# An image-and-graph kernel whose squares are taken from the rectified tile, with its engine work laid out by thirds of steps and its row gathers split anew

## The chip, the cores and the metric

The kernel runs on one core of a Trainium2 chip. The metric is the device time of one execution in microseconds (us), the median of several runs. The engines of the core work side by side and meet through semaphores: TensorE (PE in the rows, PEld for its weight loads) multiplies matrices into PSUM, VectorE (DVE) and ScalarE (ACT) do elementwise work, GpSimd (POOL) issues the row gathers through its own DMA queue, and SyncE (SP) issues the plain transfers.

## What is computed

The input is 32 images of 64 channels and 48 x 48 pixels. First comes a "convolution" by similarity, per image, then a mixture of experts whose gates come from a graph attention over all pixels. Cut to what matters:

```
xf = ln_c(x)                                            # per pixel over the 64 channels
xn = xf / |xf|
s  = relu(einsum('bcp,bcq->bpq', xn, xn)) ** 2          # 2304 x 2304 per image
g  = Wc xf + bc
x  = x + einsum('bpq,bcq->bcp', s, g)
t  = tokens of x;  n = ln_t(t)
h  = n @ W_gat                                          # 16 values per token, 4 heads
e  = leaky_relu(a_src[src] + a_dst[dst])                # 262144 edges and one loop per token
alpha = softmax of e over the edges of each dst;  agg = segment_sum(h[src] * alpha)
gates = softmax of the top 2 of 4 experts by layernorm(agg)
x  = t + sum_e gates_e * (gelu(n W1_e + b1_e) W2_e + b2_e)
```

## The kernel before

**Stages.** From 0 to about 1409 us the edges are sorted by destination (VectorE, with TensorE and ScalarE turning and copying), woven with the first 8 images. From 1409 to 3647 us run the other 24 images. Then comes the scan over the sorted edges in 32 chunks of 82 x 128 rows (to about 4255 us), a short repair of the seams, and from about 4310 us the experts, image by image.

**The image loop.** `walk` runs one `body` per image on every engine. An image has `STEPS` = 45 steps: 5 column blocks (four of 512 pixels, one of 256) times 9 pairs of row blocks. In step t TensorE writes the gram product of a pair (L1876: 8 matmuls of 64 columns, f16 high and low words) into one of two PSUM banks, ScalarE copies it rectified into SBUF as `rel` (L2066), and a third of the steps (t % 3 = 0) are squared on ScalarE (L2070), the others on VectorE (L2406: the PSUM bank times `rel`). Three steps later (`LAG`) TensorE multiplies the squares with the value rows (`values`, L1830). The bank of step t is used again in step t + 2, and TensorE waits there for whoever read it last: ScalarE's `a_rel` where ScalarE squares, VectorE's `v_s2` elsewhere. `rel` has 3 buffers, the squares have 5.

Between the steps, tied to numbers of t by small tables, stands the work of the neighbouring images: `post` and `tokens` for the image before (products for the graph features, normalisation by `spread2`, `deviation2`, `norm2`, transposes, copies), `pre`, `spread`, `deviation`, `scales`, `norm`, `units`, `high`, `low`, `turn` and `value_rows` for the image behind, `sums` for each finished column block, and in the first 16 bodies after the first the scan's move masks, `level` (L2350 to L2353, byte tiles).

**GpSimd's queue.** Independent of the images GpSimd issues 2048 gathers (L980, `gather_rows`), each 128 rows of 24 floats by a list of indices in SBUF, at most four in flight; after every 64 the rows of a chunk are stored (`store_rows`, L959). The edges only name tokens of the first 8 images, so that the gathers may run while the other 24 are computed. 48 gathers are issued before this stage (`OPENING`), the rest of `AHEAD * 64` in one go; then the queue waits for the end of the images (`img_done`). In the scan, for each chunk k, `segment_rows` fetches two large tiles (`got` L1716, `nb` L1718) and `PIECE` more gathers follow. Ahead of every fourth chunk the queue first makes sure that enough gathers are issued: `full * 64 + 10`, with `full` = 6, 11, 16, 21, 26, 31 and 32 for k = 0, 4, 8, 12, 16, 20 and 24 on, and that the stores of `full` chunks have landed. ScalarE lays `nb` and `got` out (`AE`, `GT`), VectorE runs its chain of copies and scans over them.

Of the kernel before, what the change touches and what calls it, by code (L numbers as in the profile page):

```python
# [26 lines left out]
FIRST = 8  # L27
# [1210 lines left out]
def flow(nc, n, Wc, bc, Wg, att_s, att_d, b_gat, gamma, beta, W1, b1, W2, b2):  # L1238
# [42 lines left out]
    AHEAD = 29  # L1281
    PIECE = 8
# [10 lines left out]
    with ExitStack() as ctx, ExitStack() as early, ExitStack() as late:  # L1293
# [200 lines left out]
        POST_PE = {5 + 2 * i: i for i in range(NB)}  # L1494
        POST_ACT = {6 + 2 * i: i for i in range(NB)}
        PRE_PE = {19 + 2 * i: i for i in range(NB)}
        PRE_ACT = {20 + 2 * i: i for i in range(NB)}
# [267 lines left out]
        def _(pe):  # L1765
            n.merge_tensor(pe)
            def pre(b, par, i):

                if i == 0:
                    at_least(pe, n.a_tn, NB * (b - 1))  # L1770
                else:
                    pe.wait_ge(n.a_cv, NB * b + i)
# [8 lines left out]
            def turn(b, i):  # L1781

                q0, k = TBATCH[i]
                if i == 0:
                    pe.wait_ge(n.v_lo, b + 1)
                if i >= 2:
                    pe.wait_ge(n.a_hl, NTB * b + i - 1)
# [74 lines left out]
            def body(b, own, par, nth, before, more, moved=None):  # L1862
                pe.wait_ge(n.l_in[par], 32 * (nth + 1))
                for t in range(STEPS):
                    c, k = divmod(t, PAIRS)
                    o, w = CH[c]
                    if t % 3 == 2:
                        pe.wait_ge(a_rel, STEPS * own + (t - 1))
                    else:
                        at_least(pe, v_s2, by_dve(STEPS) * own + by_dve(t - 1))  # L1870
# [12 lines left out]
                    if before and t in POST_PE:  # L1883
                        post(b - 1, 1 - par, POST_PE[t])
                    if before and t == 15:
                        tokens(b - 1, 0)
                        tokens(b - 1, 1)
                    if before and t == 17:
                        tokens(b - 1, 2)
                    if more and t in PRE_PE:  # L1890
                        if t == 19:
                            pe.wait_ge(n.x_in[1 - par], 64 * (nth + 1 + par))
                        pre(b + 1, 1 - par, PRE_PE[t])
                    if more and t == 33:
                        turn(b + 1, 0)
                        turn(b + 1, 1)
                    if more and t == 35:
# [55 lines left out]
        def _(act):  # L1953
            n.merge_scalar(act)

            def pre(b, i):
# [34 lines left out]
            def post(b, i):  # L1991
# [6 lines left out]
                for h in range(2):  # L1998
                    act.activation(c2[:, s0:s0 + k, h, :], src[:, h], ACT.Copy)
                for h in range(2):  # L2000
# [682 lines left out]
```

## Time and profile before

| | |
|---|---|
| median of 3 runs | 5282.03 us (5274.48 to 5291.11) |
| profiled execution | 5291.28 us, its span 5289.5 us |
| gathers begin | 1126.4 us |
| the 24 images, first to last gram product | 1408.8 to 3629.1 us |
| last token store of the images | 3647.2 us |
| GpSimd's first `got` of the scan | 3658.6 us |
| last of the 2048 gathers | 4102.0 us |
| `got` of chunk k = 24 | 4111.1 us |
| end of the span | 5289.5 us |

Busy shares of the span: PE 67%, VectorE 75%, ScalarE 64%, GpSimd 56%. They are averages over stages with different limits. In such a profile the question is at each meeting point who came last; an engine that is busy all the time in one stage may still have room against another queue that runs beside it through several stages.

### The profile page before, as it was taken

What the parts mean: (1) busy time and instruction counts of PE and PEld (TensorE: products, weight loads), DVE (VectorE), ACT (ScalarE), POOL (GpSimd) and SP (SyncE); (2) the same over time, 40 slices, a digit from 0 to 9 for tenths busy, and PEclk for the clock granted to TensorE, in tenths of its full rate; (3) what the DMA queues carried; (4) which work ended last, traced back from release to release, by engine and by line L of the source; (5) the groups of instructions that cost most, each with busy time, mean ns of one, the idle gap of its engine ahead of it and who ended that gap; (6) DMA issues with size and microseconds to landing.
All of it is one profiled execution on the core that took longest, in us unless ns stands there. A gap on an engine that the chain in (4) does not pass through costs nothing. (4 is left out here: it accounts for less than half of the span.)

```text
span 5289.5 us, 70597 instructions
## 1 busy us (share of the span) xinstructions
PE 3533.1 (67%) x22687; PEld 1450.6 (27%) x22687; DVE 3964.2 (75%) x5512; ACT 3392.4 (64%) x4285; POOL 2941.6 (56%) x2937
## 2 busy tenths in 40 slices
PE   4888988500488888888898988884000017788778
PEld 1223333200243344343443444342000002222222
DVE  8998988997666666766666655555999848787877
ACT  4777988401676767776676776775566526566665
POOL 6000000048777777777777777777656147666661
PEclk9999999755699999999999999997555558888889
DMA  6100100002122222222222212224555527999997
GB/s 258 36 20 20 33 21 16 17 14 82 22 47 57 42 62 48 47 52 52 56 48 46 64 40 53 48 50 105 176 190 187 190 71 147 151 161 159 155 157 141
DMA packets 332482, 441.96 MB, mean 84 GB/s; under 512 B 183193, under 2 KB 261916, under 8 KB 331500
## 3 DMA queue, kind: packets, MB, share of 16 engines
q1 hardware_dynamic: 209744, 288.12, 19.8%
q0 software_dynamic: 105536, 148.61, 16.6%
q8 instruction: 187, 3.06, 0.2%
q10 hardware_dynamic: 16896, 1.18, 0.2%
q14 instruction: 119, 0.97, 0.1%
HBM read 252.35 MB, written 166.47 MB: 79 GB/s over the span
## 5 line engine op out<-in xcount | busy, mean ns | idle before, releaser
L980 POOL DMA_INDIRECT rows<-htab_d,idx x2048 | 2134.3, 1042 | 761.3 <-issue 603.9
L2406 DVE SCALAR_TENSOR_TENSOR s<-gram,rel 128x1024 f32<-128x1024 f32 (+1 forms) x720 | 798.1, 1116 | 800.1 <-ACT rel L2066 797.3
L2066 ACT ACTIVATE rel<-gram 128x1024 f32<-128x1024 f32 (+1 forms) x1080 | 1005.4, 940 | 540.5 <-PE gram L1876 533.1
L1830 PE MATMUL acc<-s,gT 128*64 128x512 f32 (+1 forms) x4320 | 1020.2, 552 | 0.0
L1876 PE MATMUL gram<-hl 128*64 128x512 f16 (+1 forms) x4320 | 787.9, 367 | 217.5 <-DVE s L2406 182.3
L1876 PE MATMUL gram<-hl,lh 128*64 128x512 f16 (+1 forms) x4320 | 775.5, 361 | 13.5 <-issue 13.5
L1761 POOL DMA_INDIRECT R<-seg_d,nidx x576 | 587.7, 1020 | 191.3 <-issue 165.9
L1930 PE MATMUL ye<-hid,w 128*64 128x384 f32 x1536 | 376.2, 570 | 260.5 <-DVE ms L2625 195.8
L1080 POOL IOTA slots<- 64x2048 int32 x1 | 1.8, 1833 | 975.5 <-POOLq L192 975.5
L2158 ACT ACTIVATE hid<-up,b1t 128x768 f32<-128x768 f32 x384 | 333.8, 900 | 261.4 <-PE up L1942 260.1
L1876 PEld LDWEIGHTS gram<-hl 128*64 128x64 f16 x4320 | 244.5, 110 | 708.2 <-DVE s L2406 467.3
L1913 PE MATMUL tailsT<-ident,tails 128*20 128x128 f32 x24 | 5.2, 412 | 610.6 <-DVE tails L2513 610.6
L906 ACT ACTIVATE w_s2r<-w_gram 128x1024 f32<-128x1024 f32 (+1 forms) x360 | 349.4, 971 | 94.0 <-PE w_gram L775 93.5
L316 DVE TENSOR_TENSOR edges<-edges 128x2048 f32<-128x2048 f32 (+1 forms) x186 | 370.8, 1994 | 47.7 <-ACT edges L935 42.1
L1942 PE MATMUL up<-tne,w 64*128 64x384 f32 x1536 | 397.7, 599 | 3.1 <-DMA x2e<-x_d 2.5
L317 DVE TENSOR_TENSOR edges<-edges 128x2048 f32<-128x2048 f32 (+1 forms) x186 | 369.7, 1987 | 0.0
L888 ACT ACTIVATE w_s2r<-w_s2r 128x1024 f32<-128x1024 f32 (+1 forms) x360 | 362.1, 1006 | 0.0
L749 PE MATMUL w_acc<-w_s2r,w_gT 128*64 128x512 f32 (+1 forms) x1440 | 361.2, 581 | 1.1 <-ACT w_s2r L888 1.1
L2070 ACT ACTIVATE s<-rel 128x1024 f32<-128x1024 f32 (+1 forms) x360 | 349.8, 972 | 11.5
L2625 DVE SCALAR_TENSOR_TENSOR ms<-ye,b2c,gs 128x384 f32<-128x384 f32 x384 | 232.0, 616 | 152.2 <-PE up L1942 92.3
L1830 PEld LDWEIGHTS acc<-s,gT 128*64 128x64 f32 x4320 | 298.8, 138 | 155.8 <-issue 3.3
L1876 PEld LDWEIGHTS gram<-hl,lh 128*64 128x64 f16 x4320 | 246.3, 111 | 236.9 <-issue 134.5
(372 smaller groups left out, 5401.4 us busy)
## 6 DMA issues: line engine op xcount, KB each, us to landing
gs<-gates_d SPq DMA_DIRECT2D x64, 1024.0 KB
rows<-htab_d,idx POOLq DMA_INDIRECT x2048
seg_d<-state SPq DMA_DIRECT2D x32, 996.0 KB, 8.9
raw_d<-w_zeros POOLq DMA_DIRECT2D x48, 512.0 KB, 23.2
raw_d<-rows POOLq DMA_DIRECT2D x32, 768.0 KB
tne<-tn_d SPq DMA_DIRECT2D x32, 576.0 KB
x2e<-x_d SPq DMA_DIRECT2D x32, 576.0 KB
out<-res SPq DMA_DIRECT2D x64, 256.0 KB
```

Of the source, the lines that this page charges most:

```text
L316: dve.tensor_tensor(lo, a, b, ALU.min)
L317: step(dve.tensor_tensor(hi, a, b, ALU.max))
L749: last = pe.matmul(acc[(b + c) % 2][j * C:(j + 1) * C, 0:w], gT[:, b % 2, 2 * k + j, :], s2(s)[:, j * w:(j + 1) * w], start=k == 0, stop=k ...
L888: act.activation(s2(s)[:, 0:2 * w], rel(s)[:, 0:2 * w], ACT.Square).then_inc(a_s2, 1)
L980: pool.indirect_dma_start(out=n.rows[:, k % 2, j, :], out_offset=None, in_=n.htabx, in_offset=bass.IndirectOffsetOnAxis(ap=n.idx[:, g % 2, ...
L1761: pool.indirect_dma_start(out=R[:, par, j, :], out_offset=None, in_=n.seg, in_offset=bass.IndirectOffsetOnAxis(ap=nidx[:, par, j:j + 1], a ...
L1830: last = pe.matmul(acc[(par + c) % 2][j * C:(j + 1) * C, 0:w], gT[:, par, 2 * k + j, :], s2[:, u % SLOTS, j * w:(j + 1) * w], start=k == 0 ...
L1876: last = pe.matmul(bank[h * C:(h + 1) * C, j, 0:w], word[:, par, first_pixel:first_pixel + C], hl[:, par, o:o + w], start=own_words, stop= ...
L1930: last = pe.matmul(y[i % 2][h * C:(h + 1) * C, 0:EW], w2[:, k, :], hid[:, i % GROUP, h, :], start=True, stop=True)
L1942: last = pe.matmul(up[i % GROUP][:, h, 0:EW], w1[rows_, k, :], tne[rows_, par, cp * EW:(cp + 1) * EW], start=True, stop=True)
L2066: act.activation(rel[:, t % RELS, 0:2 * w].rearrange("p (j x) -> p j x", j=2), gram[(par + t) % 2][:, :, 0:w], ACT.Relu, scale=1.0 / SPLIT ...
L2406: dve.scalar_tensor_tensor(halves(s2[:, t % SLOTS, 0:2 * w]), gram[(par + t) % 2][:, :, 0:w], 1.0 / SPLIT ** 2, halves(rel[:, t % RELS, 0: ...
```

## The change

Squares: VectorE squares `rel` by itself (both inputs the same SBUF tile) in place of multiplying the PSUM bank with `rel`. With that the bank is free after ScalarE's copy, and TensorE waits for `a_rel` in every step. Order: the work beside the steps gets new places, on VectorE almost all of it at t % 3 = 0, where VectorE has no square; `sums`, `level`, `post`, `pre`, `tokens` and the rest move; `value_rows` is cut in two (`value_scaled` at t = 36, `value_rows` at t = 0 of the next body). ScalarE's `pre` and `post` copy both halves in one instruction in place of two. Gathers: `AHEAD` goes from 29 to 26 and `PIECE` from 8 to 13.

```diff
-    AHEAD = 29
-    PIECE = 8
+    AHEAD = 26
+    PIECE = 13
...
-        POST_PE = {5 + 2 * i: i for i in range(NB)}
-        POST_ACT = {6 + 2 * i: i for i in range(NB)}
-        PRE_PE = {19 + 2 * i: i for i in range(NB)}
-        PRE_ACT = {20 + 2 * i: i for i in range(NB)}
+        POST_AT = {5 + 3 * i: i for i in range(NB)}
+        PRE_AT = {14 + 3 * i: i for i in range(NB)}
...
-                    if t % 3 == 2:
-                        pe.wait_ge(a_rel, STEPS * own + (t - 1))
-                    else:
-                        at_least(pe, v_s2, by_dve(STEPS) * own + by_dve(t - 1))
+                    at_least(pe, a_rel, STEPS * own + (t - 1))
...
+                    if before and t == 23:
+                        if more:
+                            pe.wait_ge(n.a_cv, NB * (b + 2))
                         tokens(b - 1, 0)
...
                 if i == 0:
                     at_least(act, n.v_t, b)
+                    at_least(act, n.v_g, b)
...
-                for h in range(2):
-                    act.activation(dst(cv)[:, h], src[:, h], ACT.Copy)
-                for h in range(2):
-                    last = act.activation(dst(sq)[:, h], src[:, h, :, 0:C], ACT.Square)
-                last.then_inc(n.a_cv, 1)
+                act.activation(dst(cv), src, ACT.Copy)
+                act.activation(dst(sq), src[:, :, :, 0:C], ACT.Square).then_inc(n.a_cv, 1)
...
-            LEVEL_AT = {9: 0, 15: 1, 18: 2, 24: 3, 33: 4, 36: 5, 42: 6}
+            LEVEL_AT = {6: 0, 9: 1, 12: 2, 15: 3, 21: 4, 27: 5, 42: 6}
+            SUMS_AT = {12: 0, 21: 1, 33: 2, 39: 3}
...
+            def value_scaled(b):
+                dve.tensor_tensor(vr[:, :, :], cv[:, :, C:2 * C], wide(rstd[:, :]), ALU.mult).then_inc(n.pc, 1)
+
             def value_rows(b, par):
-
-                dve.tensor_tensor(vr[:, :, :], cv[:, :, C:2 * C], wide(rstd[:, :]), ALU.mult).then_inc(n.pc, 1)
                 dve.wait_ge(n.pc, b + 2)
...
                         dve.wait_ge(a_rel, STEPS * own + t + 1)
-                        halves = lambda ap: ap.rearrange("p (j x) -> p j x", j=2)
-                        dve.scalar_tensor_tensor(halves(s2[:, t % SLOTS, 0:2 * w]), gram[(par + t) % 2][:, :, 0:w], 1.0 / SPLIT ** 2,
-                                                 halves(rel[:, t % RELS, 0:2 * w]), ALU.mult, ALU.mult).then_inc(v_s2, 1)
+                        dve.tensor_tensor(s2[:, t % SLOTS, 0:2 * w], rel[:, t % RELS, 0:2 * w], rel[:, t % RELS, 0:2 * w], ALU.mult).then_inc(v_s2, 1)
...
+                    if before and t == 0:
+                        value_rows(b, par)
...
+                    if more and t == 36:
+                        value_scaled(b + 1)
```

On TensorE, in an image's body, two steps stand in a row like this before (`misc` is the bank of `pre`; the names behind "waits" are semaphores):

```order
L1876 MATMUL gram<-hl 64x512 [waits v_s2]
L1876 MATMUL gram<-hl 64x512
L1876 MATMUL gram<-hl,lh 64x512 x2
L1876 MATMUL gram<-hl 64x512 x2
L1876 MATMUL gram<-hl,lh 64x512 x2
L1824 REGISTER_ALU [waits v_s2]
L1830 MATMUL acc<-s,gT 64x512 [waits a_s2]
L1830 MATMUL acc<-s,gT 64x512
```

and now:

```order
L1872 MATMUL gram<-hl 64x512 [waits a_rel]
L1872 MATMUL gram<-hl 64x512
L1872 MATMUL gram<-hl,lh 64x512 x2
L1872 MATMUL gram<-hl 64x512 x2
L1872 MATMUL gram<-hl,lh 64x512 x2
L1822 REGISTER_ALU
L1829 MATMUL acc<-s,gT 64x512 [waits a_s2,v_s2]
L1829 MATMUL acc<-s,gT 64x512
```

The products and their number stay; the first gram product waits for ScalarE's copy, and VectorE's square is waited for only by the value products three steps later.

On VectorE, where an image's statistics are made (`ssq` is `spread`, `rstd` to `n` is `scales`, `vr` and `gT` are the value rows), before:

```order
L2406 SCALAR_TENSOR_TENSOR s<-gram,rel 128x1024 [waits a_rel]
L2267 RECIPROCAL rstd<-sd 128x18 [waits a_sd]
...
L2270 TENSOR_SCALAR n<-n 128x18 [waits v_chain]
...
L2406 SCALAR_TENSOR_TENSOR s<-gram,rel 128x1024 [waits a_rel]
L2362 TENSOR_TENSOR vr<-cv,rstd 128x1152
...
L2364 TENSOR_TENSOR gT<-vr,bcb 128x1152 [waits pc]
```

and now:

```order
L2402 TENSOR_TENSOR s<-rel 128x1024 [waits a_rel]
...
L2402 TENSOR_TENSOR s<-rel 128x1024 [waits a_rel]
L2261 RECIPROCAL rstd<-sd 128x18 [waits a_sd]
...
L2264 TENSOR_SCALAR n<-n 128x18 [waits v_chain]
L2345 TENSOR_SCALAR step_m<-step_d 128x328
...
L2402 TENSOR_TENSOR s<-rel 128x1024 [waits a_rel]
...
L2402 TENSOR_TENSOR s<-rel 128x1024 [waits a_rel]
```

The squares come in pairs and read SBUF alone; the other work stands behind each pair, and the value rows have left this place.

On GpSimd, at the end of the gathers (the row of 54 lies ahead of k = 20), before, from k = 21 on:

```order
L1716 DMA got<-raw_d,edge 128x1968
L1718 DMA nb<-htab_d,node 128x1992
L980 DMA rows<-htab_d,idx 128x24 x8
...
L980 DMA rows<-htab_d,idx 128x24 x8
L959 DMA raw_d<-rows 128x1536
L1716 DMA got<-raw_d,edge 128x1968
```

and now, from the end of k = 19 to k = 20:

```order
L980 DMA rows<-htab_d,idx 128x24 x10
L959 DMA raw_d<-rows 128x1536
L980 DMA rows<-htab_d,idx 128x24 x54
L968 TENSOR_LOAD need
L968 ISA x2
L980 DMA rows<-htab_d,idx 128x24 x10
L959 DMA raw_d<-rows 128x1536
L1714 DMA got<-raw_d,edge 128x1968
L1716 DMA nb<-htab_d,node 128x1992
L980 DMA rows<-htab_d,idx 128x24 x13
```

192 gathers have moved from ahead of the first `got` to between the chunks, 5 more to each and 70 in a row ahead of the `got` of k = 20, with the store of the 31st chunk directly ahead of it.

## Rows read from the trace of the kernel before

**Rows 1.** Head of the page.

```profile
span 5289.5 us, 70597 instructions
```

**Rows 2.** Waits of POOL: engine, line <- releaser: us in total, times, longest us.

```profile
POOL rows L980 <- issue: 603.9, 1930, 6.1
...
POOL rows L980 <- DMA rows<-htab_d,idx: 157.5, 118, 5.1
...
POOL got L1716 <- ACT GT L2111: 83.1, 6, 16.5
```

**Rows 3.** Gathers until 3411 and until 3658: count, ns min/median/max, first and last start.

```profile
L980 POOL DMA_INDIRECT rows<-htab_d,idx x1665: 942/947/7027, 1126.4 to 3411.0; - x185
...
L980 POOL DMA_INDIRECT rows<-htab_d,idx x1856: 942/947/7027, 1126.4 to 3657.4; - x186
```

**Rows 4.** Timeline at the images' end: start us, us, engine, line, operation.

```profile
3647.16 0.33 SPq L1588 DMA_DIRECT2D tn_d<-tf  x1
...
3658.60 0.95 POOL L1716 DMA_INDIRECT got<-raw_d,edge  x1 [0.30 <-issue]
```

**Rows 5.** Start of the chain that ended last: start us, us, what.

```profile
4105.51 5.55 issue
...
4111.06 0.96 POOL got L1716
...
4112.33 7.57 DMA nb<-htab_d,node
...
4119.92 1.04 ACT AE L2110
```

**Rows 6.** Gram matmuls (L1876): count, ns min/median/max, first and last start.

```profile
L1876 PE MATMUL gram<-hl x4320: 272/379/636, 1408.8 to 3629.1; 128*64 128x512 f16 x157, 128*64 128x256 f16 x40
```

**Rows 7.** Timeline, two steps of an image, TensorE.

```profile
2303.85 0.11 PEld L1876 LDWEIGHTS gram<-hl 128*64 128x64 f16 x2 [0.72 <-DVE s L2406]
...
2305.60 0.38 PE L1876 MATMUL gram<-hl 128*64 128x512 f16 x2
```

**Rows 8.** Waits, 1450 to 3600 us.

```profile
PEld gram L1876 <- DVE s L2406: 451.2, 441, 2.8
```

**Rows 9.** Groups by form, 1409 to 3632 us: count | busy us, mean ns | idle before.

```profile
L980 POOL DMA_INDIRECT rows<-htab_d,idx x1670 | 1659.1, 993 | 544.6 <-issue 484.8 <-DMA rows<-htab_d,idx 59.8
...
L2406 DVE SCALAR_TENSOR_TENSOR s<-gram,rel 128x1024 f32<-128x1024 f32 x576 | 703.1, 1223 | 749.2 <-ACT rel L2066 748.7 <-issue 0.2
```

**Rows 10.** The same, 3042 to 3632 us.

```profile
L980 POOL DMA_INDIRECT rows<-htab_d,idx x456 | 445.1, 976 | 140.1 <-issue 134.5 <-DMA rows<-htab_d,idx 5.6
```

**Rows 11.** Timeline, gathers beside VectorE's merge (L1152 to L1154 without pause).

```profile
1131.88 1.96 POOL L980 DMA_INDIRECT rows<-htab_d,idx  x1 [0.30 <-issue]
...
1131.80 1.21 DVE L1154 TENSOR_TENSOR edges<-edges 128x1024 f32<-128x1024 f32 x1
...
1135.40 1.96 POOL L980 DMA_INDIRECT rows<-htab_d,idx  x1 [0.30 <-issue]
```

**Rows 12.** Timeline, gathers beside two VectorE operations of an image.

```profile
2314.47 1.64 POOL L980 DMA_INDIRECT rows<-htab_d,idx  x1 [0.30 <-issue]
...
2313.94 1.35 DVE L2362 TENSOR_TENSOR vr<-cv,rstd 128x1152 f32<-128x1152 f32 x1
...
2303.21 0.95 POOL L980 DMA_INDIRECT rows<-htab_d,idx  x1 [0.30 <-issue]
...
2302.57 1.22 DVE L2406 SCALAR_TENSOR_TENSOR s<-gram,rel 128x1024 f32<-128x1024 f32 x1 [1.22 <-ACT rel L2066]
```

**Rows 13.** Timeline, one chunk of the scan.

```profile
3788.42 0.95 POOL L1716 DMA_INDIRECT got<-raw_d,edge  x1 [0.30 <-issue]
...
3799.88 2.79 POOL L980 DMA_INDIRECT rows<-htab_d,idx  x1 [3.94 <-DMA rows<-htab_d,idx]
...
3798.30 3.62 DVE L2505 TENSOR_TENSOR_SCAN S<-G 128x1660 f32<-128x1660 f32 x1
...
3806.89 0.96 POOL L1716 DMA_INDIRECT got<-raw_d,edge  x1 [0.30 <-issue]
```

More of the change, by code:

```diff
@@ L1769, in pre @@
                 if i == 0:
-                    at_least(pe, n.a_tn, NB * (b - 1))
+                    at_least(pe, n.a_c2, NB * (b - 1))
                 else:
@@ L1785, in turn @@
                     pe.wait_ge(n.v_lo, b + 1)
+                    at_least(pe, n.a_tn, NB * (b - 1))
                 if i >= 2:
@@ L1997, in post @@
                 src = misc[:, :, 0:k * PW].rearrange("p h (s c) -> p h s c", c=PW)
-                for h in range(2):
-                    act.activation(c2[:, s0:s0 + k, h, :], src[:, h], ACT.Copy)
-                for h in range(2):
-                    last = act.activation(sq2[:, s0:s0 + k, h, :], src[:, h, :, 0:C], ACT.Square)
-                last.then_inc(n.a_c2, 1)
+                by_half = lambda t: t[:, s0:s0 + k, :, :].rearrange("p s h c -> p h s c")
+                act.activation(by_half(c2), src, ACT.Copy)
+                act.activation(by_half(sq2), src[:, :, :, 0:C], ACT.Square).then_inc(n.a_c2, 1)
             def deviation2(b):
@@ L2070, in body @@
                         act.activation(s2[:, t % SLOTS, 0:2 * w], rel[:, t % RELS, 0:2 * w], ACT.Square).then_inc(a_s2, 1)
-                    if before and t in POST_ACT:
-                        post(b - 1, POST_ACT[t])
-                    if before and t == 12:
+                    if before and t in POST_AT:
+                        post(b - 1, POST_AT[t])
+                    if more and t in PRE_AT:
+                        pre(b + 1, PRE_AT[t])
+                    if before and t == 17:
                         deviation2(b - 1)
-                    if before and t == 16:
+                    if before and t == 23:
                         tokens(b - 1, 0)
                         tokens(b - 1, 1)
-                    if before and t == 18:
+                    if before and t == 26:
                         tokens(b - 1, 2)
-                    if more and t in PRE_ACT:
-                        pre(b + 1, PRE_ACT[t])
-                    if more and t == 26:
+                    if more and t == 25:
                         deviation(b + 1)
@@ L2085, in body @@
                         norm(b + 1)
-                    if more and t == 30:
+                    if more and t == 32:
                         high(b + 1)
-                    if more and t == 34:
+                    if more and t == 35:
                         turned(b + 1, 1 - par, 0)
                         turned(b + 1, 1 - par, 1)
-                    if more and t == 36:
+                    if more and t == 37:
                         turned(b + 1, 1 - par, 2)
@@ L2397, in norm2 @@
                 dve.tensor_tensor(hx[:, 16:18, :], c2[:, 8, :, C:PW], r[:, 8, :].unsqueeze(2).to_broadcast([P, 2, RW]), ALU.mult).then_inc(n.v_t2, 1)
+            value_scaled(FIRST)
             value_rows(FIRST, 0)
@@ L2419, in body @@
                         scales(b + 1)
-                    if more and t == 28:
-                        value_rows(b + 1, 1 - par)
-                    if more and t == 29:
+                    if more and t == 30:
                         units(b + 1)
-                    if more and t == 31:
-                        low(b + 1)
+                    if more and t == 36:
+                        value_scaled(b + 1)
                     if moved and t in LEVEL_AT:
```

30 lines of the change are left out of this document (15 added, 15 removed).

## The prediction

> **What bounds the kernel now.** (GpSimd is POOL in the rows.) I read the page first for the busy shares, then the chain that ended last, the waits of GpSimd, and the timeline at the places they name. TensorE, VectorE and ScalarE are busy nine tenths or less of the image phase and wait for each other there: TensorE lost 451 us before its gram products because VectorE still read the bank [rows 8]. It looks like the bound. The chain says otherwise. It starts at 4105.5 us in GpSimd's queue: the 25th chunk's fetch (`got`, k = 24) starts at 4111.1, its neighbour rows land 7.6 us later, ScalarE lays them out, and from there VectorE's scan chain runs to the end [rows 5]. So ask what GpSimd did until then. It issued 2048 gathers, and its idle time before them is 0.3 us of issue (603.9 us in 1930 times) and waits for landed rows (157.5 us); it waited for a consumer six times only, after the last gather [rows 2]. It never waited for an image. The images are over at 3647.2, and GpSimd takes its first `got` at 3658.6, when its 29 x 64 = 1856 gathers are issued [rows 3, 4]. **GpSimd's queue sets the time from 1126 to 4111 us; the images have 11 us to spare beside it.** A gather that nothing disturbs takes 0.95 us and 0.30 of issue: 1.25 us.
>
> **The image loop.** The change frees a gram bank after ScalarE's rectified copy instead of after VectorE's product. TensorE's own step is 1.75 us (2303.85 to 2305.60, the second start kept by no engine) [rows 7]; 36 wide steps of 1.75 and 9 half-width ones of about 0.9 make 71 us, some 7 us of other products and transposes 78. An image takes (3629.1 - 1408.8) / 24 = 92.5 us now [rows 6]. With small stalls left I estimate 82, so the images end near 1409 + 24 x 82 + 18 = 3395 (18 being 3647.2 - 3629.1, the last image's end work). That is 250 us off TensorE and nothing off the path, since GpSimd needs until 3411 for the 26 x 64 = 1664 gathers at its old pace [rows 3]. The work laid out by thirds is the same work on VectorE and TensorE, and ScalarE's merged copies move the same elements; at most a few us per image come off ScalarE. The added waits are met long before: ScalarE's first copy of an image (t = 14) waits for the value rows that VectorE now finishes at t = 0, with 14 steps between; TensorE's first token transpose (t = 23) waits for ScalarE's copy of t = 20, with the gram products of step 24 queued behind it and three steps, over 5 us, of room. SyncE's stores of an image follow five to eight steps later in unchanged order, and nothing but the last image's end work waits for them. All this I cost at nothing on the path. Its cover is the gather queue: without that, the images would bring the 250 us.
>
> **The squares.** 30 of 45 steps per image are squared on VectorE. Before, this read PSUM and one SBUF tile, 1.22 us each, 576 wide ones [rows 9]. Now it reads the SBUF tile twice. A product of two SBUF tiles of 128x1024 takes 1.21 us [rows 11], so VectorE pays nothing. GpSimd does. A gather that starts 0.64 us into the old form (2303.21 against 2302.57) still takes 0.95 us; one that starts 0.53 us into a product of two SBUF tiles (2314.47 against 2313.94) takes 1.64 and ends 0.82 us after that product [rows 12]. Beside the merge, one that starts 0.08 us in takes 1.96 and ends 0.83 us after the product [rows 11]. So a gather held inside such an operation goes on when it ends.
>
> The Trainium skill says the same on the page "SBUF — State Buffer" (Who interferes with whom): a VectorE instruction with two SBUF inputs contends with a GpSimd instruction that reads SBUF, and the loser waits in full. By that rule the squares hold gathers. The same section infers that descriptor generation needs the write side and so is not stalled by a two-tensor product; by that the squares would cost nothing (the first rival). The rows above decide between the two, and against the second.
>
> Price of one wide square to the gather queue. From below: two squares of a third sit 1.3 us apart, a held gather restarts in step, and each costs 0.03 to 0.05. From above: at steps of 1.75 a held gather restarts 2.34 us after the square's start (1.22 + 0.82 + 0.30), inside the second square, and again 1.75 later, and then 1.25 later it falls into the next third; three gathers per 5.25 us, 1.5 us lost to two squares, 0.75 each. Between: beside the merge two gathers take 3.52 us (1131.88 to 1135.40) where 2.50 would do, 1.02 lost to three operations, 0.34 each [rows 11]. And from 3042 to 3632, where no level work runs, gathers average 976 ns against 947 undisturbed [rows 3, 10]: 456 x 0.029 = 13 us for 6.4 images with five two-tile operations of 1.35 us each, 0.41 per operation. Both are near each other and of the same kind, so I take **0.35 us**. For 576 wide squares (24 images of 24) that is 202 us, for 144 half-width ones at an estimated 0.06 another 9: **+211 us** on the gather queue. Bounds: 17 to 29 us (0.03 to 0.05 x 576), and 432.
>
> So the scan may start at 3411 + 211 = **3622** instead of 3658.6, long after the images' 3395.
>
> **The scan with 13 gathers per chunk.** From `got` to `got` it takes 3806.89 - 3788.42 = 18.47 us now: ten issues of 1.25, a wait of 3.9 for rows that land behind the two large fetches, 1.9 held by the long scan, the rest small [rows 13]. Five more gathers add 6.25: 24.7 us. From below 15 x 1.25 + 3.9 = 22.7, if the hold falls within the landing wait; from above 26.5, if the long scan (3.62 us) holds a second issue. I take 24.7. VectorE's chain of 18.4 us then waits for each chunk. The counts: k = 0 to 19 take 260 gathers, to 1924; at k = 20 the code wants 31 x 64 + 10 = 1994 first, so 70 gathers stand ahead of that `got` (88 us), and the store of the 31st chunk behind them is waited for (6 us, as from 4105.5 to 4111.1 now [rows 5]); k = 20 to 23 take 52; the last two and the last store about 10. Sum: 24 x 24.7 + 88 + 6 + 4 = **691 us**, the 4 being what this last end takes beyond the one that is in today's count. Before: 4111.1 - 3658.6 = 452.5. The rest from k = 24 on is the same work in the same order.
>
> `got` of k = 24 then starts at 3622 + 691 = 4313 against 4111.1: **+202 us**. The gathers moved out of the image phase take back what the earlier start gives: 192 of them, 248 us earlier, 239 us more later. Against the profiled execution's span of 5289.5 us [rows 1] (its time is 5291.3) this gives 5491; the median of the runs shown, 5282.0, lies 9 us lower: 5282 + 202 = 5484 us.
>
> **Rivals.**
> (A) A square of one tile with itself does not hold the gathers, as a second read of the same address might not. No row shows this form with a gather inside, against it stands that every form with two SBUF inputs in the rows holds. Then the scan starts at 3411 and `got` 24 at 4102: -9 us, 5273, no measurable difference.
> (B) Faster. As A, and the hold by the long scan also falls within the landing wait, so that a chunk takes 22.7 us: 24 x 2.0 = 48 us less, 5225. It decides from a chunk period under about 24.4 us with squares that hold nothing. For it: in the landing wait GpSimd has 3.9 us per chunk to hide in. Against it: the rows of the squares' kind.
> (C) The squares hold gathers but fall in step with them at 0.05 each: 29 us instead of 211, 5302. For it: three gathers to a pair of squares can settle; against it the two groups of rows that measured 0.34 and 0.41.
> (D) The images do not shorten, because ScalarE or the new third-steps take the place of the wait. Then they end at 3647, GpSimd's 3622 is no longer last, and the scan starts at about 3650: +230 us, 5512.
>
> **How the numbers follow.** Forecast 0.74; A 0.10, B 0.05, C 0.05, D 0.06. Within the forecast the price per square is open from about 0.15 (-115 us) to 0.55 (+115), the chunk period by -48 and +43. D is inside. A range from 5340 to 5620 holds forecast and D up to a tail of 0.04 at each side of what I believe and leaves out A, B and C. Differences under 0.3% (16 us) can't be told by a measurement of this kernel. Faster by more: B, with a sliver of A, 0.06. Within: most of A and a little of C, 0.11. Slower by more: the forecast, D and most of C, 0.83.
>
> **What the changed profile would show.** Images: last gram matmul near 3380, TensorE hardly waiting for VectorE. Squares: mean gather above 1.2 us in the image phase (993 ns now), gathers that start inside a square ending 0.82 us after it. GpSimd's first `got` near 3620, more than 150 us after the last token store. Scan: `got` to `got` near 24.7 us, a gap of some 115 us before k = 20, `got` 24 near 4313, and the same 1178 us from there to the end. Wrong would be: gathers of 0.95 us inside squares (A), a first `got` right behind the images (D), or a chain that no longer passes through `got` 24.

## The result and the profile after

The changed kernel takes **5382.7 us** (median; 5372.2 to 5386.9) against 5282.9 us of the kernel before in the same session: a ratio of **1.0186**, interval 1.0163 to 1.0209. That is +100 us, in the forecast's direction and inside its range (5340 to 5620), but just under half of the +202 us forecast. The profiled spans differ by 5385.1 - 5289.5 = 95.6 us; the sums below are made against that.

Below, the head of the profile's page of after (the changed kernel), and the group of its gathers (line, engine, operation, count | busy us, mean ns | idle before):

```profile
span 5385.1 us, 70993 instructions
...
PE 3496.0 (65%) x22687; PEld 1480.6 (27%) x22687; DVE 3978.8 (74%) x5512; ACT 3384.7 (63%) x3997; POOL 3125.7 (58%) x2937
...
L980 POOL DMA_INDIRECT rows<-htab_d,idx x2048 | 2288.9, 1118 | 661.9 <-issue 606.6
```

The busy shares are those of before to two points, and the kernel is 96 us longer. What the shares do not show is the length of a gather, which is looked at below.

**The images** are shorter, as forecast. Gram matmuls of after (count, ns min/median/max, first and last start), then its waits from 1450 to 3380 us (engine, line <- releaser: us in total, times, longest):

```profile
L1872 PE MATMUL gram<-hl x4320: 272/379/636, 1409.0 to 3391.6; 128*64 128x512 f16 x157, 128*64 128x256 f16 x40
```

```profile
DVE s L2402 <- ACT rel L2060: 430.3, 413, 8.0
PEld gram L1872 <- issue: 423.0, 1274, 3.6
POOL rows L980 <- issue: 397.2, 1297, 1.9
ACT rel L2060 <- PE gram L1872: 263.4, 463, 7.0
...
PEld gram L1872 <- ACT rel L2060: 26.4, 72, 0.9
```

(3391.6 - 1409.0) / 24 = 82.6 us per image, 92.5 before [rows 6]. TensorE waited 451 us for VectorE's squares [rows 8]; of that wait no row is left, and 26 us for ScalarE's copy have come in its place.

**The gathers of the image phase** are slower. Groups of after, 1409 to 3392 us, and its 1664 gathers ahead of the first `got`:

```profile
L980 POOL DMA_INDIRECT rows<-htab_d,idx x1378 | 1526.8, 1108 | 441.0 <-issue 408.8 <-DMA rows<-htab_d,idx 32.2
...
L2402 DVE TENSOR_TENSOR s<-rel 128x1024 f32<-128x1024 f32 (+1 forms) x718 | 791.6, 1121 | 461.7 <-ACT rel L2060 447.4 <-issue 1.9
```

```profile
L980 POOL DMA_INDIRECT rows<-htab_d,idx x1664: 938/947/6402, 1126.8 to 3545.4; - x185
```

A gather takes 1108 ns on average where it took 993 [rows 9]; the median has not moved (947), so most run undisturbed and some are held. The last of the 1664 starts at 3545.4 instead of 3409.7, one place ahead of the 1665th at 3411.0 in [rows 3]. Timeline of after, the last token store of the images and the first `got` (start us, us, engine, line, operation [idle before <- releaser]):

```profile
3409.34 0.33 SPq L1586 DMA_DIRECT2D tn_d<-tf  x1
...
3546.61 0.94 POOL L1714 DMA_INDIRECT got<-raw_d,edge  x1 [0.31 <-issue]
```

The images are done 137 us before GpSimd asks for them, and it asks without a wait. Before, the two lay 11 us apart [rows 4].

**The scan.** The chain that ended last in after, 4190 to 4215 us (start us, us, what), and the waits from 3546 to 4204 us:

```profile
4200.27 3.73 issue
4204.01 0.96 POOL got L1714
...
4205.27 7.58 DMA nb<-htab_d,node
...
4212.87 1.03 ACT AE L2104
```

```profile
ACT AE L2104 <- DMA nb<-htab_d,node: 381.9, 24, 128.0
DVE AE L2481 <- ACT AE L2104: 329.7, 24, 129.7
...
POOL rows L980 <- DMA rows<-htab_d,idx: 15.6, 17, 2.2
```

The chain is that of before, 93 us later: `got` of k = 24 at 4204.0 instead of 4111.1 [rows 5]. In all 24 chunks VectorE now waits for ScalarE, which waits for the fetch; in before this happened once, for 1.6 us. From k = 24 to the end it takes 1181.1 us, 1178.4 before. So 93 of the 96 us lie ahead of `got` 24: it took 657.4 us from the first `got` where it took 452.5 (+204.9), and the first `got` came 112.0 earlier.

### The profile page after: what moved, and what is told of

Read it like the earlier page. It is cut to its first block and busy times, and to the rows that moved or that the text cites. A ratio compares the mean times of both kernels' runs of the same rounds, so it can differ in the third digit from the quotient of the medians.

```text
span 5385.1 us, 70993 instructions
## 1 busy us (share of the span) xinstructions
PE 3496.0 (65%) x22687; PEld 1480.6 (27%) x22687; DVE 3978.8 (74%) x5512; ACT 3384.7 (63%) x3997; POOL 3125.7 (58%) x2937
## 5 line engine op out<-in xcount | busy, mean ns | idle before, releaser
L980 POOL DMA_INDIRECT rows<-htab_d,idx x2048 | 2288.9, 1118 | 661.9 <-issue 606.6
L2402 DVE TENSOR_TENSOR s<-rel 128x1024 f32<-128x1024 f32 (+1 forms) x720 | 792.9, 1119 | 463.0 <-ACT rel L2060 448.7
L1829 PE MATMUL acc<-s,gT 128*64 128x512 f32 (+1 forms) x4320 | 1037.7, 555 | 22.5 <-DVE s L2402 22.5
L1872 PE MATMUL gram<-hl 128*64 128x512 f16 (+1 forms) x4320 | 800.8, 365 | 47.3 <-issue 39.2
L1872 PE MATMUL gram<-hl,lh 128*64 128x512 f16 (+1 forms) x4320 | 792.7, 362 | 0.0
L1872 PEld LDWEIGHTS gram<-hl 128*64 128x64 f16 x4320 | 256.4, 111 | 386.0 <-issue 232.4
L2481 DVE COPY_PREDICATED AE<-moveg,AE 128x72 f32<-128x72 uint8 (+6 forms) x224 | 101.7, 454 | 347.3 <-ACT AE L2104 340.7
## 6 DMA issues: line engine op xcount, KB each, us to landing
raw_d<-w_zeros POOLq DMA_DIRECT2D x48, 512.0 KB, 23.3
```

Of the source, the lines that this page charges most:

```text
L980: pool.indirect_dma_start(out=n.rows[:, k % 2, j, :], out_offset=None, in_=n.htabx, in_offset=bass.IndirectOffsetOnAxis(ap=n.idx[:, g % 2, ...
L1829: last = pe.matmul(acc[(par + c) % 2][j * C:(j + 1) * C, 0:w], gT[:, par, 2 * k + j, :], s2[:, u % SLOTS, j * w:(j + 1) * w], start=k == 0 ...
L1872: last = pe.matmul(bank[h * C:(h + 1) * C, j, 0:w], word[:, par, first_pixel:first_pixel + C], hl[:, par, o:o + w], start=own_words, stop= ...
L2402: dve.tensor_tensor(s2[:, t % SLOTS, 0:2 * w], rel[:, t % RELS, 0:2 * w], rel[:, t % RELS, 0:2 * w], ALU.mult).then_inc(v_s2, 1)
```

## The experiments

All times are medians of runs beside the kernel before on the same chip (5290.4, 5285.4 or 5292.0 us); a ratio is given with its interval, and where there is none the time is a single run. In the expectations H is the theory of the prediction (GpSimd's queue is the bound, and the squares hold it), S its rival by which the gathers moved between the chunks are the whole loss; the other letters are explained where they stand. They were made after the result above was known, each ahead of its own run. "Mean gather" is that from 1409 to 3380 us, and an instant is read from one profiled execution. In each, the 1664th gather and the first `got` are the two instants to compare.

### Only the squares, in the old order (squares_only)

Against before:

```diff
-                    if t % 3 == 2:
-                        pe.wait_ge(a_rel, STEPS * own + (t - 1))
-                    else:
-                        at_least(pe, v_s2, by_dve(STEPS) * own + by_dve(t - 1))
+                    at_least(pe, a_rel, STEPS * own + (t - 1))
...
-                        dve.scalar_tensor_tensor(halves(s2[:, t % SLOTS, 0:2 * w]), gram[(par + t) % 2][:, :, 0:w], 1.0 / SPLIT ** 2,
-                                                 halves(rel[:, t % RELS, 0:2 * w]), ALU.mult, ALU.mult).then_inc(v_s2, 1)
+                        dve.tensor_tensor(s2[:, t % SLOTS, 0:2 * w], rel[:, t % RELS, 0:2 * w], rel[:, t % RELS, 0:2 * w], ALU.mult).then_inc(v_s2, 1)
```

> The kernel before with one part of the change: VectorE squares the rectified SBUF tile and TensorE waits for ScalarE's copy in every step; old order of the other work, 29 chunks ahead, 8 gathers between. Theory H (a gather waits out a VectorE product of two SBUF tiles; the gather queue sets the time): the hold stays, about 0.22 us per wide square, so the 1857th position of the gather queue (the first got of the scan) moves from 3659 us to about 3795, the chunk period stays 18.5 us, time about 5283 + 136 = 5419. Rival S (the gathers moved between the chunks are what costs; the squares only free TensorE): first got at 3650 to 3659, time 5283 or a little less.

Measured: 5413.9 us, 1.0237 (1.0213 to 1.0261). Mean gather 1096 ns; the 1664th starts at 3536.7; first `got` at 3782.2, 236 us after the last gram product (3546.3). The squares alone cost 124 us, by holding a queue that none of their operands touches, though they shorten the images (89.1 us each). The hold does not need the new order or the new split. The instants of the 1664th gather carry some noise: with the old order and the old squares it starts at 3409.7 in before, 3401.3 in before_28_10 and 3394.2 in split_only, three kernels that do the same work up to there.

### Only the split 26 / 13 (split_only)

```diff
-    AHEAD = 29
-    PIECE = 8
+    AHEAD = 26
+    PIECE = 13
```

> The kernel before with only the numbers of gathers changed: 26 chunks ahead, 13 between. H: the images end at 3647 as before and now set the first got (about 3650); the scan to the got of chunk 24 takes 657 us as in the changed kernel (452.5 before): got 24 at 4307, time 5283 + 196 = 5479. Rival S says slower too, by the same 205 us less the earlier start; a rival that takes a gather as equally dear in both places expects the same time as before, since the queue has the same 2048 gathers.

Measured: 5492.1 us, 1.0389 (1.0369 to 1.0410). The 1664 gathers are out at 3394.2, and then GpSimd has nothing it may do:

```profile
3645.31 0.94 POOL L1716 DMA_INDIRECT got<-raw_d,edge  x1 [249.67 <-SPq L1633]
```

250 us of the bounding queue lie idle while the images end. The split by itself is a loss of 202 us; it is only worth something behind shorter images.

### The new order and the split, with the old squares (psum_squares)

Against after: the square reads the PSUM bank times `rel` again, and TensorE waits for `v_s2` as before.

```diff
-                    at_least(pe, a_rel, STEPS * own + (t - 1))
+                    if t % 3 == 2:
+                        pe.wait_ge(a_rel, STEPS * own + (t - 1))
+                    else:
+                        at_least(pe, v_s2, by_dve(STEPS) * own + by_dve(t - 1))
...
-                        dve.tensor_tensor(s2[:, t % SLOTS, 0:2 * w], rel[:, t % RELS, 0:2 * w], rel[:, t % RELS, 0:2 * w], ALU.mult).then_inc(v_s2, 1)
+                        dve.scalar_tensor_tensor(halves(s2[:, t % SLOTS, 0:2 * w]), gram[(par + t) % 2][:, :, 0:w], 1.0 / SPLIT ** 2,
+                                                 halves(rel[:, t % RELS, 0:2 * w]), ALU.mult, ALU.mult).then_inc(v_s2, 1)
```

> The changed kernel with the squares put back: VectorE reads the PSUM bank and the rectified tile, TensorE waits for VectorE again; new order, merged copies, 26 and 13 stay. H: gathers are no longer held by squares (mean near 0.99 us in the image phase against 1.108), the 1665th near 3411; the images slow down again to between 84 and 92 us each and set the first got, somewhere between 3440 and 3640; then 657 us to the got of chunk 24. Time 5283 - 14 to 5283 + 187, by where the images end. Rival S: 5383 as the changed kernel or more.

Measured: 5358.7 us, 1.0131 (1.0103 to 1.0159). Groups from 1409 to 3380 us and the first `got`:

```profile
L980 POOL DMA_INDIRECT rows<-htab_d,idx x1488 | 1464.6, 984 | 489.2 <-issue 433.6 <-DMA rows<-htab_d,idx 55.5
```

```profile
3507.50 0.94 POOL L1714 DMA_INDIRECT got<-raw_d,edge  x1 [113.60 <-SPq L1631]
```

The mean is back at 984 ns and the 1664th gather starts at 3393.0, 152 us earlier than in after. That is what the squares hold in this order (with 28 and 29 chunks ahead, psum_28_11 and after_29_8 below, the same pair of instants is 3388.5 and 3539.8, 151 us apart). It is the net delay of the queue: the gathers themselves are 166 us longer in all, and some 20 of that are taken from the waits for landed rows. But the images take 86.6 us here, so the queue waits 114 us for them. The first `got` comes 39 us earlier than in after and `got` 24 37 us; the stretch from there to the end is 16 us longer (1197 against 1181 us; it lies between 1178 and 1197 in the traces here, and why was not followed up), and the time falls by 24 us only. The bound changes hands between the two kernels, which is why neither the shorter images nor the free queue shows its worth alone.

### VectorE rectifies, ScalarE squares (swapped)

Against after, in the steps with t % 3 != 0 (the waits of ScalarE and TensorE are turned to match, `rel` is still written and read in SBUF, the squares are the same numbers):

```diff
-                        dve.wait_ge(a_rel, STEPS * own + t + 1)
-                        dve.tensor_tensor(s2[:, t % SLOTS, 0:2 * w], rel[:, t % RELS, 0:2 * w], rel[:, t % RELS, 0:2 * w], ALU.mult).then_inc(v_s2, 1)
+                        dve.wait_ge(pe_gram, STEPS * own + t + 1)
+                        at_least(dve, a_s2, STEPS * own + (t - RELS + 1))
+                        dve.tensor_scalar(rel[:, t % RELS, 0:2 * w].rearrange("p (j x) -> p j x", j=2), gram[(par + t) % 2][:, :, 0:w],
+                                          0.0, 1.0 / SPLIT ** 2, ALU.max, ALU.mult).then_inc(v_s2, 1)
...
+                        act.wait_ge(v_s2, by_dve(STEPS) * own + by_dve(t + 1))
+                    act.activation(s2[:, t % SLOTS, 0:2 * w], rel[:, t % RELS, 0:2 * w], ACT.Square).then_inc(a_s2, 1)
```

> The changed kernel with the two engines' parts exchanged in two of three steps: VectorE rectifies the PSUM bank into SBUF (one input, in PSUM), ScalarE squares the SBUF tile; TensorE's bank is free after the rectified copy as in the change, the sizes and the number of elementwise operations stay. H: no VectorE operation of a step has two SBUF inputs, so gathers run at a mean near 0.98 us in the image phase, the images keep about 83 us each, the first got comes near 3415 and the got of chunk 24 near 4072: time about 5245, faster than both kernels. Rival S (split) or a rival by which any VectorE traffic in SBUF slows the gathers: about 5383 as the changed kernel.

Measured: 5306.0 us, 1.0035 (1.0021 to 1.0050): 61 us above what was expected. Mean gather 996 ns, so a one-input read from PSUM holds no more than the old squares did, and the 1664th starts at 3405.9. The miss is in the images: 84.9 us each, not 83, and the first `got` waits 60 us for them:

```profile
3466.95 0.94 POOL L1714 DMA_INDIRECT got<-raw_d,edge  x1 [60.15 <-SPq L1631]
```

The expectation had taken the image length of after for a form that waits elsewhere. From that `got` to the one of k = 24 it takes 655.7 us, 657.4 in after: that stretch goes with the split 26 / 13 and not with the form of the squares.

### One square of a pair from PSUM (first_psum, second_psum)

In each third of steps VectorE squares twice in a row, t % 3 = 1 and 2. Here one of the two keeps the old form: t % 3 = 1 in first_psum (the diff shows this one), t % 3 = 2 in second_psum. In the expectations this separates theory P (a lone square costs as much as the first of a pair, and the second of a pair is nearly free) from its rival L (each square costs the same, so half of them hold half as much). For the bank that VectorE reads TensorE waits for VectorE again.

```diff
-                        dve.tensor_tensor(s2[:, t % SLOTS, 0:2 * w], rel[:, t % RELS, 0:2 * w], rel[:, t % RELS, 0:2 * w], ALU.mult).then_inc(v_s2, 1)
+                        if t % 3 == 1:
...
+                            dve.scalar_tensor_tensor(halves(s2[:, t % SLOTS, 0:2 * w]), gram[(par + t) % 2][:, :, 0:w], 1.0 / SPLIT ** 2,
+                                                     halves(rel[:, t % RELS, 0:2 * w]), ALU.mult, ALU.mult).then_inc(v_s2, 1)
+                        else:
+                            dve.tensor_tensor(s2[:, t % SLOTS, 0:2 * w], rel[:, t % RELS, 0:2 * w], rel[:, t % RELS, 0:2 * w], ALU.mult).then_inc(v_s2, 1)
```

> The changed kernel, but the first square of each pair (t % 3 = 1) reads the PSUM bank and the rectified tile as before, and TensorE waits for VectorE for that bank; only the second square of a pair has two SBUF inputs (12 wide ones per image instead of 24). Theory P (a square costs by how a gather meets it: the first of a pair meets one at random, the second follows 1.2 to 1.45 us later, just when the held gather's successor starts, and costs little): a lone square is a first one, about 0.42 us each, so the 1664th gather is issued near 3399 + 288 x 0.42 = 3520, most of the way to the 3545 of the changed kernel. Rival L (each square costs the same 0.25): half way, near 3472.

> The changed kernel, but the second square of each pair (t % 3 = 2) reads the PSUM bank and the rectified tile, the first has two SBUF inputs. P: as with the other half, 1664th gather near 3520. L: near 3472. If only the first squares of pairs cost anything by themselves, this one is near 3520 and the one before it near 3400.

Measured:

| | two-SBUF wide squares | mean gather, ns | 1664th gather | over psum_squares | per wide square |
|---|---|---|---|---|---|
| psum_squares | 0 | 984 | 3393.0 | | |
| first_psum | 288 | 1068 | 3503.2 | +110 | 0.38 us |
| second_psum | 288 | 1079 | 3511.4 | +118 | 0.41 us |
| after | 576 | 1109 | 3545.4 | +152 | 0.26 us |

(The half-width squares, a quarter as many, are left aside in the division.) Half of the squares cost nearly three quarters of the whole. A lone square costs 0.4 us, its partner 0.12 to 0.15 more. The two single runs carry the noise named above, some 15 us; L's 76 us for half of the squares lies outside it. Timelines of second_psum and of after, POOL and DVE:

```profile
2405.08 1.99 POOL L980 DMA_INDIRECT rows<-htab_d,idx  x1 [0.30 <-issue]
...
2405.04 1.22 DVE L2410 TENSOR_TENSOR s<-rel 128x1024 f32<-128x1024 f32 x1 [0.49 <-ACT rel L2063]
```

```profile
2405.99 1.15 POOL L980 DMA_INDIRECT rows<-htab_d,idx  x1 [0.30 <-issue]
2407.45 0.94 POOL L980 DMA_INDIRECT rows<-htab_d,idx  x1 [0.30 <-issue]
...
2405.10 2.42 DVE L2402 TENSOR_TENSOR s<-rel 128x1024 f32<-128x1024 f32 x2
```

Above, a gather meets a lone square at its start: it loses 1.05 us and ends 0.81 after it (2405.04 + 1.22 = 2406.26; 2405.08 + 1.99 = 2407.07). Below, two squares in a row from 2405.10 to 2407.52: the first ends near 2406.31, the gather inside it ends 0.83 later at 2407.14, *during* the second square and not after it, and the next one starts at 2407.45, when the second is all but over. The gather is not held a second time, and the issue of 0.30 fills what is left of the pair.

That the two stand back to back is not the reason by itself. In squares_only 108 of 264 second squares start about 2.4 us after the first, and there the second is nearly free too. Timeline of squares_only, POOL and DVE:

```profile
2103.23 1.23 DVE L2402 TENSOR_TENSOR s<-rel 128x1024 f32<-128x1024 f32 x1 [0.70 <-ACT rel L2063]
2103.46 1.81 POOL L980 DMA_INDIRECT rows<-htab_d,idx  x1 [0.30 <-issue]
...
2105.58 0.96 POOL L980 DMA_INDIRECT rows<-htab_d,idx  x1 [0.30 <-issue]
2105.64 1.22 DVE L2402 TENSOR_TENSOR s<-rel 128x1024 f32<-128x1024 f32 x1
```

The first square holds a gather until 2105.27; the next gather starts 0.06 us *ahead* of the second square and is not held. What a gather loses goes by where it starts: in second_psum those that start up to 0.7 us ahead of a lone square take 0.94 us (median), those that start 0.1, 0.5 and 1.0 us into it 1.94, 1.52 and 1.05. After a held gather the next one starts 2.34 us behind the start of the square (1.22 + 0.82 + 0.30). So where the second square comes 1.1 to 1.4 us behind the first, that gather starts when most of the second is over; at 1.8 it starts 0.5 us into it and is held; at 2.4 it starts just ahead of it and is not. Taking all wide pairs from 1409 to 3380 us, with the time over 0.947 us of each gather that ends 0.7 to 0.9 us after a square as that square's hold:

| second square behind the first | pairs | held by the first | by the second |
|---|---|---|---|
| after, under 1.5 us | 280 | 0.40 us | 0.13 us |
| squares_only, under 1.5 us | 61 | 0.40 us | 0.17 us |
| squares_only, 1.5 to 2.2 us | 29 | 0.72 us | 0.62 us |
| squares_only, 2.2 to 2.6 us | 108 | 0.31 us | 0.03 us |

(In the 66 pairs of squares_only that lie further apart the second holds 0.26 us.)

### The split on the kernel before, 28 / 10 (before_28_10)

```diff
-    AHEAD = 29
-    PIECE = 8
+    AHEAD = 28
+    PIECE = 10
```

> The kernel before with 28 chunks ahead and 10 gathers between. It measures the chunk period of the scan with two more gathers. Theory V (the 18.47 us of before were VectorE's own pace, and GpSimd's own pace with 8 gathers was shorter, hidden by its hold at the long scan: 23.2 - 5 x 1.25 = 17.0): with 10 gathers 19.5 us. Rival, the step of the prediction (each gather adds 1.25 us to 18.47): 21.0. First got at the images' end, 3650; got of chunk 24 by V near 3650 + 24 x 19.5 + 8 = 4126, time near 5298; by the rival near 4162 and 5334.

Measured: 5335.9 us. From k = 0 to 19 a chunk takes 19.5 us on average (18.3 to 23.0), with 8 gathers 18.5 [rows 13]. That is V's figure: two more gathers cost 0.5 each, not 1.25. The time is nevertheless 50 us up, close to the rival's figure, for other reasons. One was overlooked in the expectation: 28 x 64 + 24 x 10 = 2032 gathers, so 16 are left over, and the interval ahead of `got` 24 is 45.5 us, 26 more than a period; `got` 24 comes at 4145.7. And from there to the end it takes 10 us more than in before (1188 against 1178). The period, not the time, decides here.

### The change with the old split (after_29_8)

Against after:

```diff
-    AHEAD = 26
-    PIECE = 13
+    AHEAD = 29
+    PIECE = 8
```

> The changed kernel with the old numbers of gathers, 29 chunks ahead and 8 between. H: the squares hold gathers until the images end at 3410; 192 more gathers then pass at 1.25 us, first got near 3545 + 240 = 3786, chunk period 18.5, got of chunk 24 near 4238, time near 5283 + 130 = 5413: the new split saves the change some 30 us, it does not cost it any. Rival S (the split is the loss): near 5283.

Measured: 5413.9 us, 1.0247 (1.0227 to 1.0266), first `got` at 3782.5, then 18.5 us per chunk. The split thus saves the change 31 us against its own old split, while it costs the kernel before 202: the images are finished early (last token store at 3407.2), so that with fewer gathers ahead the scan can start earlier, and of the gathers that are moved behind the first `got` a part hides beside VectorE's chain. With the old split the shorter images bring nothing: the first `got` waits for no image.

### Two versions against both kernels (psum_28_11, swapped_27_14)

psum_squares waited 114 us for the images, swapped 60. Both get more gathers ahead, to fill that wait: psum_28_11 is psum_squares with the edit below, swapped_27_14 is swapped with 27 and 14 in their places.

```diff
-    AHEAD = 26
-    PIECE = 13
+    AHEAD = 28
+    PIECE = 11
```

> The changed kernel with VectorE's squares from PSUM again (TensorE waits for VectorE), with 28 chunks ahead and 11 gathers between. With 26 ahead the images ended at 3507 and GpSimd stood idle from 3394 on; 128 more gathers ahead take it to about 3394 + 160 = 3554. V: chunk period 17.0 + 3 x 1.25 = 20.7, no run of gathers ahead of chunk 20, got of chunk 24 near 3556 + 24 x 20.7 + 8 = 4061, 50 us earlier than in the kernel before: time near 5283 - 48 = 5235, faster than both. Rival (each gather adds to 18.47: 22.2 per chunk): 4097 and 5270.

> The kernel with the engines' parts exchanged (VectorE rectifies from PSUM, ScalarE squares), with 27 chunks ahead and 14 gathers between. First got near 3406 + 80 = 3486 with the images over at 3467. V: chunk period 17.0 + 6 x 1.25 = 24.5, no run ahead of chunk 20, got of chunk 24 near 3486 + 24 x 24.5 + 8 = 4082: time near 5283 - 26 = 5257. Rival (the change's 23.2 at 13 gathers, then 1.25 more per gather, is the same; a rival with VectorE's pace as floor only expects no less): 5250 to 5270.

Measured: psum_28_11 **5223.1 us** (5219.7 to 5229.3), **0.9871** (0.9851 to 0.9892): 69 us faster than before and 160 faster than the change. swapped_27_14 5248.7 us, 0.9924 (0.9906 to 0.9942). Timeline and waits (3555 to 4038 us) of psum_28_11:

```profile
3555.65 0.94 POOL L1714 DMA_INDIRECT got<-raw_d,edge  x1 [0.30 <-issue]
...
4038.67 1.10 POOL L1714 DMA_INDIRECT got<-raw_d,edge  x1 [3.73 <-issue]
```

```profile
ACT AE L2107 <- DMA nb<-htab_d,node: 130.3, 24, 37.0
```

The queue never waits for the images, whose last gram product is at 3491.0; a chunk takes 20.4 us (k = 0 to 19; V had 20.7), in swapped_27_14 24.6 (V: 24.5); and since 28 x 64 + 24 x 11 is over 2048, no row of gathers stands ahead of `got` 20 or 24. The first `got` comes 103 us earlier than in before, and 31 us of that are spent again on 11 gathers per chunk in place of 8: `got` 24 at 4038.7 is 72 us earlier.

## Why the forecast had the direction right and twice the size

Terms of the sum, as the prediction put them:

| term | forecast | measured |
|---|---|---|
| images: length, last token store | 82 us, 3395 | 82.6 us, 3409.3 |
| first `got` | 3622 | 3546.6 |
| chunk period | 24.7 us | 23.2 us |
| gap of `got` 19 to 20 beyond a period | 94 us | 94 us |
| first `got` to `got` 24 | 691 us | 657.4 us |
| `got` 24 | 4313 (+202) | 4204.0 (+93) |
| from there to the end | as before | +2.7 us |

**The bound** was right. The first `got` waits for nothing, and the chain runs through `got` 24 in both. That the queue and not the images sets the start of the scan is shown in after_29_8, where the images end 240 us earlier than in before and the kernel is 2.5% slower, and in after, where 137 us lie between the last token store and the first `got`. That the bound changes hands close by is shown in psum_squares: with a queue freed by 152 us the images take over.

**The images** were right in length. They bring nothing with the old split; behind the new one they are what lets the first `got` come at 3546.6, where split_only has to wait until 3645.3. Which part shortens them the experiments split: 92.5 us before, 89.1 with the new squares alone, 86.6 with the order and the merged copies alone, 82.6 with both; order and copies were not separated.

**A square of one tile with itself** (rival A) holds gathers like two different tiles: gathers end 0.8 us after it, and squares_only gives 1096 ns. The rule of the Trainium skill ("SBUF — State Buffer", Who interferes with whom), that a VectorE instruction with two SBUF inputs contends with a GpSimd instruction that reads SBUF, makes no exception for one tile read twice, and the trace agrees; the inference in the same section that descriptor generation would be spared is not borne out here, for gathers whose indices lie in SBUF.

**First failed step: 0.35 us per wide square.** The prediction took this price from two groups of rows, 0.34 and 0.41 per operation, and gave it to every square alike. 0.41 fits a lone square (0.38 and 0.41 measured) or the first of a pair (0.40). But the 30 squares of an image come in pairs, t % 3 = 1 and 2, the second nearly always 1.1 to 1.45 us behind the first (281 of 288 wide pairs), and it holds only 0.13 more. The prediction had both numbers of this geometry, the distance of 1.3 us in its lower bound and the restart at 2.34 us in its upper one, and did not put them together: the gather that restarts finds 0.2 us of the second square left. The upper bound put the squares 1.75 us apart, where the rows of squares_only do show a dear second square. A pair costs the queue 0.53 us, 0.26 per square, the half-width ones left aside: 152 us against psum_squares, where the forecast had 211, so the price is 59 us too large. Against before the 1664th gather is 136 us late, and the term is 75 us off, of the 109 us by which `got` 24 was missed. The rest, some 16 us, is that psum_squares already runs the queue 17 us faster than before (3393.0 against 3409.7). Whether the new order does that is not shown, as split_only is at 3394.2 in the old order.

**Second failed step: five more gathers add 6.25 us to 18.47.** The prediction carried over the wait of 3.9 us for landed rows and the hold of 1.9 unchanged. From k = 1 to 19 the wait fell from 3.9 us per chunk in before to 0.5 in after, and the holds (the time of GpSimd's instructions over 0.95 us) rose from 2.1 to 4.1: 6.0 beside ten issues became 4.6 beside fifteen, and 15 x 1.25 + 4.6 is 23.3. Over k = 0 to 19 the kernels here have 18.5 us at 8 gathers, 19.5 at 10, 20.4 at 11, 23.2 at 13 and 24.6 at 14: the first added gathers cost 0.5 each, the last 1.4. V, the theory recorded ahead of before_28_10, gives 19.5, 20.7 and 24.5 for 10, 11 and 14 from the 23.2 at 13: 18.47 us was the pace of VectorE's chain (18.4), which in before waits for its input once in 24 chunks (waits from 3658 to 4111 us) and in after every time, 330 us in all:

```profile
DVE AE L2484 <- ACT AE L2110: 1.6, 1, 1.6
```

No row shows the queue waiting for VectorE there. The one link that the rows show is the hold by the long scan; that this is what keeps the queue in VectorE's step is argued, not tested. In after's chunks the hold by the long scan falls where the landing wait was:

```profile
3708.16 0.94 POOL L1714 DMA_INDIRECT got<-raw_d,edge  x1 [0.30 <-issue]
3709.41 2.18 POOL L1716 DMA_INDIRECT nb<-htab_d,node  x1 [0.31 <-issue]
3711.90 3.29 POOL L980 DMA_INDIRECT rows<-htab_d,idx  x1 [0.30 <-issue]
3715.49 0.95 POOL L980 DMA_INDIRECT rows<-htab_d,idx  x1 [0.30 <-issue]
...
3710.81 3.62 DVE L2502 TENSOR_TENSOR_SCAN S<-G 128x1660 f32<-128x1660 f32 x1
```

The gather of 3711.9 is held until 3715.19, and while it is held the rows ahead of it land: the next one follows without the 3.9 us of [rows 13]. Rival B had this overlap, with 22.7 as its figure; 23.2 lies near it, though what is left in the chunk is hold and not, as B had it, the landing wait. The scan to `got` 24 took 691 - 657 = 34 us less than forecast (24 x 1.5 = 36), and with the 75 this makes up the 109.

**Rivals.** A and D are out: the mean gather is 1108 ns, where A would leave it near the 993 of before, and the images did shorten. C, by which all squares fall in step with the gathers at 0.05 each, holds nearly for the second square of a pair (0.13) and not for the first (0.40). Half of B is right, with A's half wrong. The price and the period both lay within what the prediction had left open (from 0.15 us, from -48 us), and both below the value it took, because each was read from rows of another pattern.

**Still open.** More than four gathers in flight, which might shorten the queue's landing waits (158 us in before [rows 2]), was not tried. Why the images take 84.9 us in swapped was read from the waits (TensorE for `rel` of ScalarE and of VectorE) and not tested. Why the stretch from `got` 24 to the end differs by up to 19 us from trace to trace is open.

## What to carry to other kernels

A queue that never waits for its consumer, and that its consumer waits for, is the bound however low its busy share is; making its partner faster brings nothing until the queue's own part ahead of the meeting point is made shorter. Price a contention by the pattern in which the operations come, not by one operation's loss: ask where the held instruction's successor starts, and what stands there. A second operation may cost next to nothing, or as much as the first. And before adding to a loop's period, ask whose pace the period is: the first additions go into the slack of whoever was not setting it.

## What the runs showed of the chip

- A VectorE product that reads one SBUF tile twice holds GpSimd's indirect gathers as one that reads two tiles. A gather caught in it ends 0.8 us after it. The same product with one operand in PSUM (mean gather 984 ns), or a one-input operation from PSUM (996 ns), doesn't.
- A gather that starts ahead of such a square is not held (0.94 us); one that starts 0.1, 0.5 or 1.0 us into it takes 1.94, 1.52 or 1.05 us (medians of second_psum).
- The hold does not add up over two squares in a row: 0.38 to 0.41 us for a lone 1.22 us square, 0.53 for a pair 1.1 to 1.45 us apart. The gather caught in the first ends during the second. 2.4 us apart the second costs as little (0.03), 1.5 to 2.2 us apart it costs 0.62 (squares_only).
- The scan operation of 3.62 us also holds a gather (3.29 us in place of 0.95), but rows of earlier gathers land meanwhile (waits for them: 0.5 us per chunk in after, 3.9 in before), so that its cost is less than what the gather's length shows.
